# A graph attention layer on one core: p and the turned one-hots as float32r words in two parts, in place of three bf16 parts

## The chip, the cores and the metric
The kernel runs on one core of one Trainium2 chip. A core has five engines with instruction streams of their own: TensorE (PE; its weight loads are listed as PEld), VectorE (DVE), ScalarE (ACT), GpSimd (POOL) and SyncE (SP), which here only issues DMAs. They meet through semaphores. The metric is the device time of one execution in microseconds, lower is better.

## The reference
One layer over a graph of 12500 nodes with 256 features and 200000 edges (src, dst, weight), with 4 heads of 64 features. For each head:

```python
feats = jnp.maximum(x @ w1 + bb1, 0.0) @ w2 + bb2
x_cat = jnp.concatenate([feats[row], feats[col], elem[:, None]], axis=1)   # 64 + 64 + 1 = 129
hid = jnp.maximum(x_cat @ a1 + aab1, 0.0)
e1 = leaky_relu((hid @ a2 + aab2)[:, 0], 0.2)
w = jnp.exp(e1 - jnp.max(e1))
pooled = segment_sum(w[:, None] * feats[col], row, n)
row_sum = segment_sum(w, row, n) + 1e-10
return pooled / row_sum[:, None]
```

The heads are put side by side, added to x, and each row is normalised. Everything is float32.

## The kernel before, in words
The product with a1 is split. For each node the kernel makes p = feats @ a1[0:64] + ab1 (the part of the source node, 4 heads x 129 = 516 numbers, `ZW`) and q = feats @ a1[64:128] (of the destination). For an edge, hid is then relu(p[src] + q[dst] + weight * a1[128]).

**Set-up and sort stage** (up to about 1500 us). Edges are sorted by window: the source node number modulo 100 is the window (`W` = 100 windows of `WN` = 125 nodes). DVE makes one-hots of places (`chunks`, L1433) and row numbers (`row_ids`, L1442, L1447), PE multiplies them, POOL scatters the rows to memory (L695). Woven into the same loop by the lists `beside` and `order`, PE makes the node products, and for each window DVE adds the bias to p (`p_sum`, L1454), and POOL splits the f32 row of p into three bf16 rows that add up to it (`split_p`: cast L706, subtract L708, cast L711, subtract L713); SP stores them in `p_table` (L527), q and feats in `qf_table`.

**A passage** (1500 to some 1560 us). DVE makes small tables on one partition: `win_pack` (the window of each tile, four to a word) and `end_prev` (how many tiles must be done before a window of p may be overwritten), L1502 to L1511. It also splits the weight row a1[128] in three parts (`a_parts`, L1479 to L1487), which SP puts under each window of p as rows 125 to 127. PE turns the sorted records in 13 groups (L939), ACT and DVE take them, and ACT sets the accumulator `acc` to zero in 13 pieces (L1147). SP then loads the first records (L581) and raises `s_start`, for which PE, ACT, DVE and POOL wait.

**Tile loop** (to about 4700 us). 1664 tiles of 128 edges, 8 to a step, 3 steps to a body, in the order that `step` of each engine writes out. Per tile:
- POOL gathers the 128 rows of q and feats by an indirect DMA (L754).
- ACT builds the one-hot of each edge's source row in its window, with the edge weight in three bf16 parts in columns 125 to 127 (`onehots`, L1193 to L1197). PE turns it (`turn`, L984, in halves of four tiles), and ACT copies the turned half from PSUM to `onehot_t` as bf16 (`take_turned`, L1182).
- PE picks p[src] + weight * a1[128] by `onehot_t` times the three parts of the window `p_win`: three matmuls for each of two halves of 258 columns (`hidden_src`, L971). For the second half it also adds the gathered q in f32 (L975).
- DVE adds the q of the first half (L1558) and makes the four dots with a2 (L1568); once per step it makes the running maximum with PE's help (L1590, PE L990, L1594, PE L995, L1604).
- ACT scales the gathered feats by exp (`weight`, L1164, four per tile), PE sums them by source row with the unturned one-hot in f32 (`sum_up`, L958), and DVE adds the sums to `acc` (L1617).

PSUM has two buffers for the sums of p and q, two for L958's and one for the turn. SP reloads the two slots of `p_win` in turn: it waits until the tiles of the window before last are done (`s_z_mm`), loads (L594), waits for the landing (L595) and raises `s_win_ready`.

**Finish** (the last 130 us): division, x added, normalisation, output.

Of the kernel before, what the change touches and what calls it, by code (L numbers as in the profile page):

```python
# [25 lines left out]
I32 = mybir.dt.int32  # L26
BF16 = mybir.dt.bfloat16
AX_X = mybir.AxisListType.X


def gnn_layer(nc, x, src, dst, weight, W1, b1, W2, b2, A1, ab1, A2, ab2, out):
# [50 lines left out]
    p_table = nc.dram_tensor("p_table", (N, 3 * ZW), BF16, kind="Internal").ap()  # L82
# [7 lines left out]
    with ctx:  # L90
# [12 lines left out]
        ones_b = sb("ones_b", [P, P], BF16)  # L103
        before = sb("before", [P, P], BF16)
        iota_row = sb("iota_row", [P, WN])
        iota_win = sb("iota_win", [P, CH, W], BF16)
# [4 lines left out]
        onehot_t = sb("onehot_t", [P, SB, P], BF16)  # L111
# [13 lines left out]
        end_prev = sb("end_prev", [1, W], I32)  # L125
        win_pack = sb("win_pack", [1, NT // 4], I32)
# [4 lines left out]
        row_tmp = onehot_t[0:1, :, :].rearrange("p t n -> p (t n)").bitcast(I32)[:, 0:NT // 4]  # L131
        assert NT <= RING * P
# [17 lines left out]
        h_t = carve(MC * NG).rearrange("p (m n) -> p m n", m=MC)  # L150
        f_t = carve(2 * NG).rearrange("p (q n) -> p q n", q=2)
        p_f = carve(2 * ZW).rearrange("p (b n) -> p b n", b=2)
        p_out = carve(2 * 3 * ZW // 2).bitcast(BF16).rearrange("p (b n) -> p b n", b=2)
        qf_acc = carve(3 * QW)
        a_row = carve(ZW)
        a_rest = carve(ZW)
        a_parts = carve(3 * ZW // 2 + 2).bitcast(BF16)[:, 0:3 * ZW]
# [10 lines left out]
        hi_oh = carve(2 * HB * HI // 2).bitcast(BF16).rearrange("p (b c n) -> p b c n", b=2, c=HB)  # L168
        lo_oh = carve(2 * HB * LO // 2).bitcast(BF16).rearrange("p (b c n) -> p b c n", b=2, c=HB)
        same_col = carve(HCOL * LO).rearrange("p (c n) -> p c n", c=HCOL)  # L170
# [25 lines left out]
        base_lo = base_hl[:, CB * W // 2:].bitcast(BF16)  # L196
        edge_row = base_hl[:, 0:EC]
# [19 lines left out]
        before_f = carve_z(P)  # L217
        counts = carve_z(W)
# [13 lines left out]
        step_p = carve_z(3 * (W + 1)).bitcast(BF16).rearrange("p (u n) -> p u n", u=3)  # L232
        assert used_z[0] <= RING * QW
# [7 lines left out]
        p_flat = p_win[:, :, :].rearrange("p a n -> p (a n)")  # L241
        shift_flat = shift_all[:, :, :].rearrange("p s h -> p (s h)")
# [48 lines left out]
        s_acc_zero = sem("s_acc_zero")  # L291

# [13 lines left out]
        s_p_rest = sem("s_p_rest")  # L306
        s_p_mid = sem("s_p_mid")
# [175 lines left out]
        def _(sp):  # L483
# [71 lines left out]
            for v in range(2):  # L555
                for a, b in ROWS:
                    sp.dma_start(p_win[a:b, v, :], p_w[0:1, v, a:b, :].rearrange("a p n -> (a p) n")).then_inc(s_win[v], 16)
            sp.wait_ge(s_a_step, 5)
            for slot in range(2):
                for r in range(3):  # L560
                    sp.dma_start(p_win[WN + r:WN + r + 1, slot, :], a_parts[0:1, :]).then_inc(s_a_rows, 16)
# [17 lines left out]
            sp.wait_ge(s_tab_step, N_TAB_STEPS)  # L579
            sp.wait_ge(s_rec_st, 16 * BULK)  # L580
# [7 lines left out]
            with sp.Fori(1, W // 2) as g:  # L588
                for v in range(2):
# [3 lines left out]
                    for a, b in ROWS:  # L593
                        sp.dma_start(p_win[a:b, v, :], p_w[bass.ds(g, 1), v, a:b, :].rearrange("a p n -> (a p) n")).then_inc(s_win[v], 16)  # L594
# [24 lines left out]
        def _(pool):  # L619
# [5 lines left out]
            pool.memset(ones_b[:, :], 1.0).then_inc(s_const, 1)  # L625
# [5 lines left out]
            pool.iota(iota_win[:, :, :], [[0, CH], [1, W]], base=0, channel_multiplier=0, allow_small_or_imprecise_dtypes=True).then_inc(s_const, 1)  # L631
# [7 lines left out]
            pool.affine_select(out=before[:, :], in_=ones_b[:, :], pattern=[[1, P]], compare_op=ALU.is_ge,  # L639
# [4 lines left out]
            pool.tensor_copy(before_f, before[:, :]).then_inc(s_const, 1)  # L644
# [13 lines left out]
            pool.affine_select(out=before[:, :], in_=before[:, :], pattern=[[0, P]], compare_op=ALU.is_ge,  # L658
# [40 lines left out]
            def split_p(g, w):  # L699
# [86 lines left out]
        def _(pe):  # L786
# [158 lines left out]
            def step(i, k):  # L945
# [15 lines left out]
                def hidden_src(j):  # L961
# [67 lines left out]
        def _(act):  # L1029
# [16 lines left out]
            def windows(g, b, j):  # L1046
# [3 lines left out]
                for c in range(j * CH, (j + 1) * CH):  # L1050
                    op = act.activation(win_oh[0:EP, b % 2, c, :], iota_win[0:EP, 0, :], ACT.Abs, scale=-1.0,  # L1051
                                        bias=edge_win[0:EP, bass.ds((g * PER + b) * CB + c, 1)])
# [679 lines left out]
```

## Time and profile before

| | us |
|---|---|
| time, median of 3 runs | 4868.68 (4866.79 to 4869.52) |
| span of the profiled execution | 4828.3 |
| DVE busy | 4460.2 (92%) |
| PE busy | 4260.4 (88%) |
| ACT busy | 3835.5 (79%) |
| POOL busy | 2693.5 (56%) |

The profiled execution is known by its span, from its first to its last instruction; the time of a run also has what lies around that. Matmuls overlap in PE's pipeline, so the sum of their durations is more than PE's busy time. An f32 product shows as two entries (x2), a bf16 one as one. Line numbers are those of the kernel before.

### The profile page before, as it was taken

How to read it: one execution, taken by the hardware profiler on the slowest of the kernel's cores; microseconds unless marked ns; L12 is line 12 of the kernel's file. 1: busy time of each engine (PE TensorE's matmuls, PEld its weight loads, DVE VectorE, ACT ScalarE, POOL GpSimd, SP SyncE). 2: the span in 40 equal slices, each digit the busy share in tenths (PEclk: the TensorE clock that was granted, in tenths of full speed). 3: DMA queues.
4: the chain of work that ended last, by engine and by line, in shares of the span. 5: the costliest groups of instructions: out<-in, count | busy, mean ns of one | idle time of the engine just before them, and what ended most of it. 6: DMA issues, size and time to landing. Idle time of an engine off the chain costs nothing.

```text
span 4828.3 us, 133194 instructions
## 1 busy us (share of the span) xinstructions
PE 4260.4 (88%) x24114; PEld 3004.1 (62%) x24115; DVE 4460.2 (92%) x25378; ACT 3835.5 (79%) x12983; POOL 2693.5 (56%) x2886
## 2 busy tenths in 40 slices
PE   1598998898896999999999999999999999999990
PEld 1355555555555777777777777777777777777760
DVE  8799999999996999999999999999999999999998
ACT  1587778778774888888888888888888888888884
POOL 5366666666664555555555555555555555555544
PEclk9999999999997999999999999999999999999995
DMA  2133333333334877777777777777777777777757
GB/s 85 43 73 86 79 71 80 81 77 80 79 76 137 240 225 221 228 225 224 224 225 224 225 225 221 226 224 224 225 224 224 224 225 225 225 225 225 221 172 212
DMA packets 266918, 851.82 MB, mean 176 GB/s; under 512 B 107916, under 2 KB 109584, under 8 KB 266861
## 3 DMA queue, kind: packets, MB, share of 16 engines
q0 software_dynamic: 169920, 673.54, 50.0%
q1 hardware_dynamic: 63543, 160.18, 11.2%
q10 hardware_dynamic: 33398, 17.49, 1.4%
q8 instruction: 18, 0.29, 0.0%
q14 instruction: 39, 0.32, 0.0%
HBM read 739.10 MB, written 111.90 MB: 176 GB/s over the span
## 4 chain that ended last, share of the span: by engine, by line
PE 36%; ACT 27%; issue 3%; DVE 2%; DMA 1%; ACTq 0%; POOL 0%; DVEq 0%; SPq 0%; POOLq 0%
ACT z L1164 18%; PE psum L971 15%; PE psum L975 9%; PE psum L958 8%; ACT onehot L1193 3%; ACT onehot_t L1182 3%; PE psum L984 3%; ACT onehot L1197 2%; PE psum L939 1%; DVE z L1689 1%; DVE z L1682 0%; PE psum L995 0%; ACT onehot L1195 0%; DVE z L1705 0%; DMA p_win<-p_table 0%
## 5 line engine op out<-in xcount | busy, mean ns | idle before, releaser
L754 POOL DMA_INDIRECT z<-qf_table,rec x1664 | 1609.2, 967 | 1454.9 <-PE psum L958 1027.1
L1164 ACT ACTIVATE z<-z 128x64 f32<-128x64 f32 x6656 | 1651.1, 335 | 0.0
L971 PE MATMUL psum<-p_win,onehot_t 128*128 x9984 | 1407.8, 274 | 84.1 <-ACT onehot_t L1182 68.3
L971 PEld LDWEIGHTS psum<-p_win,onehot_t 128*128 128x128 bf16 x9984 | 966.8, 97 | 540.0 <-issue 214.4
L958 PE MATMUL psum<-z,onehot 128*128 128x260 f32 x3328 | 1029.4, 391 | 6.7 <-DVE acc L1617 4.9
L975 PE MATMUL psum<-z,ident 128*128 128x258 f32 x3328 | 1002.7, 383 | 0.0
L1568 DVE SCALAR_TENSOR_TENSOR z<-z,a_b 128x129 f32<-128x129 f32 x3328 | 884.3, 290 | 5.6 <-issue 0.2
L1568 DVE SCALAR_TENSOR_TENSOR z<-psum,a_b 128x129 f32<-128x129 f32 x3328 | 828.2, 286 | 0.0
L1558 DVE TENSOR_TENSOR z<-z,psum 128x258 f32<-128x258 f32 x1664 | 698.6, 420 | 94.6 <-PE psum L975 90.6
L1617 DVE TENSOR_TENSOR acc<-acc,psum 125x260 f32 x1664 | 702.3, 422 | 25.3 <-PE psum L958 2.4
L695 POOL DMA_INDIRECT sorted_rows<-z x300 | 478.5, 1595 | 403.9 <-DVE z L1447 321.6
L958 PEld LDWEIGHTS psum<-z,onehot 128*128 128x128 f32 x3328 | 575.8, 190 | 103.1 <-DVE acc L1617 27.7
L1182 ACT ACTIVATE onehot_t<-psum 128x512 bf16<-128x512 f32 x416 | 243.4, 585 | 437.7 <-PE psum L984 437.7
L1193 ACT ACTIVATE onehot<-iota_row,rec 128x125 f32<-128x125 f32 x1664 | 525.5, 389 | 26.3 <-PE psum L958 22.7
L1051 ACT ACTIVATE z<-iota_win,z 125x100 bf16<-125x100 bf16 x1600 | 470.3, 369 | 71.3 <-DMA base_rows<-z 56.3
L1433 DVE TENSOR_SCALAR acc<-z 125x320 bf16<-125x320 bf16 x1600 | 521.1, 388 | 0.3 <-issue 0.3
L975 PEld LDWEIGHTS psum<-z,ident 128*128 128x128 f32 x3328 | 502.2, 190 | 20.3
L857 PE MATMUL psum<-acc 128*128 128x500 f32 x800 | 377.8, 594 | 5.6 <-ACT acc L1085 5.6
L1398 DVE SCALAR_TENSOR_TENSOR z<-psum,z 125x100 f32<-125x100 f32 x1600 | 319.5, 253 | 24.1 <-PE psum L823 24.0
L984 PE MATMUL psum<-ident,onehot 128*128 128x128 f32 x1664 | 261.5, 280 | 55.7 <-ACT onehot L1197 55.7
L1197 ACT ACTIVATE onehot<-onehot,ones_f 128x500 f32<-128x500 f32 x416 | 298.2, 717 | 0.0
L1091 ACT ACTIVATE acc<-psum,acc 128x500 f32<-128x500 f32 x200 | 135.3, 676 | 196.0 <-PE psum L857 195.9
(220 smaller groups left out, 5576.3 us busy)
## 6 DMA issues: line engine op xcount, KB each, us to landing
p_table<-acc SPq DMA_DIRECT2D x100, 338.6 KB
p_win<-p_table SPq DMA_DIRECT2D x100, 338.6 KB
z<-qf_table,rec POOLq DMA_INDIRECT x1664, 4.5
qf_table<-acc SPq DMA_DIRECT2D x75, 339.5 KB
acc<-in_x_dram SPq DMA_DIRECT2D x25, 448.0 KB
z<-in_x_dram SPq DMA_DIRECT2D x20, 560.0 KB
out_dram<-z ACTq DMA_DIRECT2D x20, 560.0 KB
qf_table<-z SPq DMA_DIRECT2D x25, 339.5 KB
```

The source lines that it names most:

```text
L695: pool.indirect_dma_start(out=sorted_rows, out_offset=bass.IndirectOffsetOnAxis(ap=row_i[0:KB[k], (b - 3) % 2, k:k + 1], axis=0), in_=rows ...
L754: pool.indirect_dma_start(out=z_t[:, o + j, :], out_offset=None, in_=qf_table, in_offset=bass.IndirectOffsetOnAxis(ap=rec[:, o + j, 3:4].b ...
L958: pe.matmul(psum[:, 4 + j % 2, 0:H * HF], onehot[:, slot, :], z_t[:, slot, ZW:QW], start=True, stop=True)\
L971: mm = pe.matmul(to, onehot_t[:, j, :], p_flat[:, bass.ds((w % 2) * (3 * ZW) + (part * ZW + o), n)], start=(part == 0), stop=(part == 2 an ...
L975: mm = pe.matmul(z_two(slot), ident[:, :], z_t[:, slot, NA:ZW], start=False, stop=True, skip_group_check=True)
L1051: op = act.activation(win_oh[0:EP, b % 2, c, :], iota_win[0:EP, 0, :], ACT.Abs, scale=-1.0, bias=edge_win[0:EP, bass.ds((g * PER + b) * CB ...
L1164: op = act.activation(z_t[:, slot, o:o + DO], z_t[:, slot, o:o + DO], ACT.Copy, scale=z_t[:, slot, o + DO:o + HF])
L1193: op = act.activation(onehot[:, oo + j, 0:WN], iota_row[:, :], ACT.Abs, scale=-1.0, bias=rec[:, oo + j, 0:1])
L1433: op = dve.tensor_scalar(chunk_oh[0:EP, r, c, :], iota_k[0:EP, :], chunk_f[0:EP, c:c + 1], None, ALU.is_equal)
L1558: dve.tensor_tensor(own, own, z_one(slot), ALU.add).then_inc(s_z_added, 1)
L1568: return dve.scalar_tensor_tensor(out=own, in0=of, scalar=0.0, in1=a2_b[:, h * AT:(h + 1) * AT], op0=ALU.max, op1=ALU.mult, accum_out=e_ra ...
L1617: dve.tensor_tensor(a, a, psum[0:WN, 4 + j % 2, 0:H * HF], ALU.add).then_inc(s_acc, 1)
```

## The change
The three bf16 parts of p become two f32 words, written as float32r; the turned one-hot is stored as float32r too, and the matmul of each half runs over two parts. `p_table` and `p_win` hold 2 x 516 words of four bytes in a row (4128 bytes) where they held 3 x 516 of two (3096). POOL splits p by one cast and one subtract, DVE the weight row likewise. To make room, tables and constants move: `ones_b`, `before` and `iota_win` into space in z, the digit one-hots into that of h_t, and `win_pack` and `end_prev` are made in z and then stored by one DMA into partition 125 of `acc`, after ACT has zeroed it.

```diff
-        p_win = sb("p_win", [P, 2, 3 * ZW], BF16)
+        p_win = sb("p_win", [P, 2, 2 * ZW], F32R)
-        onehot_t = sb("onehot_t", [P, SB, P], BF16)
+        onehot_t = sb("onehot_t", [P, SB, P], F32R)
-        end_prev = sb("end_prev", [1, W], I32)
-        win_pack = sb("win_pack", [1, NT // 4], I32)
+        tables = acc[WN:WN + 1, 0:NT // 4 + W].bitcast(I32)
+        win_pack = tables[:, 0:NT // 4]
+        end_prev = tables[:, NT // 4:NT // 4 + W]
...
             sp.wait_ge(s_a_rows, 16 * 6)
             sp.wait_ge(s_tab_step, N_TAB_STEPS)
+            sp.wait_ge(s_acc_zero, 1 + BULK)
+            sp.dma_start(tables, made).then_inc(s_tab_st, 16)
+            sp.wait_ge(s_tab_st, 16)
             sp.wait_ge(s_rec_st, 16 * BULK)
...
-                pool.tensor_copy(p_out[0:WN, b, 0:ZW], pf).then_inc(s_p_hi, 1)
+                pool.tensor_copy(p_out[0:WN, b, 0:ZW].bitcast(F32R), pf).then_inc(s_p_hi, 1)
                 pool.wait_ge(s_p_hi, n + 1)
-                pool.tensor_tensor(pf, pf, p_out[0:WN, b, 0:ZW], ALU.subtract).then_inc(s_p_rest, 1)
-                pool.wait_ge(s_p_rest, n + 1)
-                pool.sem_inc(s_passed, 1)
-                pool.tensor_copy(p_out[0:WN, b, ZW:2 * ZW], pf).then_inc(s_p_mid, 1)
-                pool.wait_ge(s_p_mid, n + 1)
-                pool.tensor_tensor(p_out[0:WN, b, 2 * ZW:3 * ZW], pf, p_out[0:WN, b, ZW:2 * ZW], ALU.subtract).then_inc(s_p_lo, 1)
+                pool.tensor_tensor(p_out[0:WN, b, ZW:2 * ZW].bitcast(F32R), pf, p_out[0:WN, b, 0:ZW], ALU.subtract).then_inc(s_p_lo, 1)
...
-                        for part in range(3):
-                            mm = pe.matmul(to, onehot_t[:, j, :], p_flat[:, bass.ds((w % 2) * (3 * ZW) + (part * ZW + o), n)],
-                                           start=(part == 0), stop=(part == 2 and not (o and PEH)), skip_group_check=True)
+                        for part in range(2):
+                            mm = pe.matmul(to, onehot_t[:, j, :], p_flat[:, bass.ds((w % 2) * (2 * ZW) + (part * ZW + o), n)],
+                                           start=(part == 0), stop=(part == 1 and not (o and PEH)), skip_group_check=True)
...
-            dve.tensor_copy(ap3[:, 0, :], ar).then_inc(s_a_step, 1)
+            dve.tensor_copy(ap2[:, 0, :].bitcast(F32R), ar).then_inc(s_a_step, 1)
             dve.wait_ge(s_a_step, 1)
-            dve.tensor_tensor(rest, ar, ap3[:, 0, :], ALU.subtract).then_inc(s_a_step, 1)
-            dve.wait_ge(s_a_step, 2)
-            dve.tensor_copy(ap3[:, 1, :], rest).then_inc(s_a_step, 1)
-            dve.wait_ge(s_a_step, 3)
-            dve.tensor_tensor(rest, rest, ap3[:, 1, :], ALU.subtract).then_inc(s_a_step, 1)
-            dve.wait_ge(s_a_step, 4)
-            dve.tensor_copy(ap3[:, 2, :], rest).then_inc(s_a_step, 1)
+            dve.tensor_tensor(ap2[:, 1, :].bitcast(F32R), ar, ap2[:, 0, :], ALU.subtract).then_inc(s_a_step, 1)
```

## Rows read from the trace of the kernel before

**Rows 1.** The page, part 1: busy us (share of the span) x instructions.
```profile
PE 4260.4 (88%) x24114; PEld 3004.1 (62%) x24115; DVE 4460.2 (92%) x25378; ACT 3835.5 (79%) x12983; POOL 2693.5 (56%) x2886
```

**Rows 2.** Busy time by stage: stretch, its length, engines, PEclk, DMA share, GB/s.
```profile
200.00:1500.00 1300.00, 1152.51 (x4726) 661.03 (x4724) 1232.94 (x6178) 1004.52 (x2716) 826.85 (x696) 0.97 0.36 79
...
1600.00:4700.00 3100.00, 2966.46 (x18665) 2244.95 (x18665) 2898.40 (x18268) 2653.40 (x9860) 1681.98 (x2044) 1.00 0.76 223
```

**Rows 3.** The page, part 4: the chain that ended last, by engine.
```profile
PE 36%; ACT 27%; issue 3%; DVE 2%; DMA 1%; ACTq 0%; POOL 0%; DVEq 0%; SPq 0%; POOLq 0%
```

**Rows 4.** The chain in order of time, 3002 to 3018: start, us, what.
```profile
3009.05 0.52 PE psum L984 x4
...
3014.43 0.66 PE psum L971 x6
3015.09 0.44 PE psum L975 x2
...
3017.06 0.45 PE psum L984 x4
...
3017.61 0.60 ACT onehot_t L1182
```

**Rows 5.** ACT in order of time, 3002 to 3009: start, us [idle before].
```profile
3002.54 0.60 ACT L1182 ACTIVATE onehot_t<-psum 128x512 bf16<-128x512 f32 x1 [2.19 <-PE psum L984]
...
3008.14 0.72 ACT L1197 ACTIVATE onehot<-onehot,ones_f 128x500 f32<-128x500 f32 x1
```

**Rows 6.** Groups, 1600 to 4700: busy us, mean ns | idle before, releaser.
```profile
L971 PEld LDWEIGHTS psum<-p_win,onehot_t 128*128 128x128 bf16 x9840 | 952.1, 97 | 528.5 <-issue 207.3
...
L975 PEld LDWEIGHTS psum<-z,ident 128*128 128x128 f32 x3282 | 494.7, 190 | 20.1
...
L1182 ACT ACTIVATE onehot_t<-psum 128x512 bf16<-128x512 f32 x409 | 239.2, 585 | 420.5 <-PE psum L984 420.5
L984 PEld LDWEIGHTS psum<-ident,onehot 128*128 128x128 f32 x1636 | 188.1, 141 | 141.0 <-ACT onehot L1197 119.3 <-issue 0.3
```

**Rows 7.** Groups of DVE alone, 1600 to 4700.
```profile
L1558 DVE TENSOR_TENSOR z<-z,psum 128x258 f32<-128x258 f32 x1641 | 688.9, 420 | 81.0 <-PE psum L975 77.5 <-issue 0.5
...
L1594 DVE TENSOR_REDUCE head_max<-psum 4x1 f32<-4x128 f32 x206 | 57.1, 277 | 64.6 <-PE psum L990 64.6
```

**Rows 8.** Waits of SP, 1600 to 4600: us in total, times, longest.
```profile
SPq L594 <- PE psum L975: 2209.6, 96, 26.1
SPq L596 <- DMA p_win<-p_table: 499.5, 97, 6.4
```

**Rows 9.** Groups in the sort stage, 200 to 1500.
```profile
L1433 DVE TENSOR_SCALAR acc<-z 125x320 bf16<-125x320 bf16 x1576 | 515.5, 389 | 0.3 <-issue 0.3
...
L1442 DVE SCALAR_TENSOR_TENSOR z<-z 128x101 f32<-128x101 f32 x300 | 118.0, 441 | 7.2 <-ACT z L1079 7.1
L708 POOL TENSOR_TENSOR acc<-acc 125x516 f32<-125x516 f32 x100 | 115.4, 1154 | 8.3
L713 POOL TENSOR_TENSOR acc<-acc 125x516 bf16<-125x516 f32 x100 | 112.6, 1126 | 8.0
...
L711 POOL CAST acc<-acc 125x516 bf16<-125x516 f32 x100 | 61.9, 619 | 16.8 <-POOL acc L708 16.8
```

**Rows 10.** L1433 and L1442 in 200 to 1500: ns min/median/max.
```profile
L1433 DVE TENSOR_SCALAR acc<-z x1576: 286/298/1231, 199.7 to 1488.5; 125x320 bf16<-125x320 bf16 x197
...
L1442 DVE SCALAR_TENSOR_TENSOR z<-z x300: 308/316/1252, 217.2 to 1497.4; 128x101 f32<-128x101 f32 x150
```

**Rows 11.** POOL and DVE in order of time, 702 to 704.
```profile
702.72 1.10 POOL L713 TENSOR_TENSOR acc<-acc 125x516 bf16<-125x516 f32 x1
702.82 1.12 DVE L1442 SCALAR_TENSOR_TENSOR z<-z 128x101 f32<-128x101 f32 x1
```

**Rows 12.** ACT in order of time, 1550 to 1556.
```profile
1550.49 1.85 ACT L1147 ACTIVATE acc<-zero_col 128x2000 f32<-128x2000 f32 x1
```

**Rows 13.** The chain in order of time, its longest pieces.
```profile
1551.74 2.00 DMA records<-z
```

More of the change, by code:

```diff
@@ L27 @@
 BF16 = mybir.dt.bfloat16
+F32R = mybir.dt.float32r
 AX_X = mybir.AxisListType.X
@@ L81, in gnn_layer @@
     qf_table = nc.dram_tensor("qf_table", (N, QW), F32, kind="Internal").ap()
-    p_table = nc.dram_tensor("p_table", (N, 3 * ZW), BF16, kind="Internal").ap()
+    p_table = nc.dram_tensor("p_table", (N, 2 * ZW), F32, kind="Internal").ap()
     CHUNKS = NT * P // S
@@ L196, in gnn_layer @@
         base_lo = base_hl[:, CB * W // 2:].bitcast(BF16)
+        assert NT // 4 + W <= CB * W
+        made = base_hl[0:1, 0:NT // 4 + W].bitcast(I32)
+        made_pack = made[:, 0:NT // 4]
+        made_end = made[:, NT // 4:NT // 4 + W]
         edge_row = base_hl[:, 0:EC]
@@ L217, in gnn_layer @@
         before_f = carve_z(P)
+        ones_b = carve_z(P // 2).bitcast(BF16)
+        before = carve_z(P // 2).bitcast(BF16)
+        iota_win = carve_z(W // 2).bitcast(BF16)
         counts = carve_z(W)
@@ L624, in _ @@
             pool.memset(ones_f[:, :], 1.0).then_inc(s_const, 1)
-            pool.memset(ones_b[:, :], 1.0).then_inc(s_const, 1)
+            pool.memset(ones_b, 1.0).then_inc(s_const, 1)
             pool.memset(ident[:, :], 0.0).then_inc(s_const, 1)
@@ L630, in _ @@
             pool.iota(iota_row[:, :], [[1, WN]], base=1, channel_multiplier=0, allow_small_or_imprecise_dtypes=True).then_inc(s_const, 1)
[L631 removed]
+            pool.iota(iota_win, [[1, W]], base=0, channel_multiplier=0, allow_small_or_imprecise_dtypes=True).then_inc(s_const, 1)
             pool.iota(iota_k, [[1, KC_MAX]], base=-(KC_MAX // 2), channel_multiplier=0, allow_small_or_imprecise_dtypes=True).then_inc(s_const, 1)
@@ L637, in _ @@
                                fill=1.0, base=0, channel_multiplier=1).then_inc(s_const, 1)
-            pool.affine_select(out=before[:, :], in_=ones_b[:, :], pattern=[[1, P]], compare_op=ALU.is_ge,
+            pool.affine_select(out=before, in_=ones_b, pattern=[[1, P]], compare_op=ALU.is_ge,
                                fill=0.0, base=-1, channel_multiplier=-1).then_inc(s_const, 1)
@@ L643, in _ @@
             pool.tensor_copy(ident_b, ident[:, :]).then_inc(s_const, 1)
-            pool.tensor_copy(before_f, before[:, :]).then_inc(s_const, 1)
+            pool.tensor_copy(before_f, before).then_inc(s_const, 1)
             pool.affine_select(out=same_col, in_=ones_f[:, 0:HCOL * LO].rearrange("p (c n) -> p c n", c=HCOL), pattern=[[-HI, HCOL], [0, LO]],
@@ L657, in _ @@
             pool.wait_ge(s_const, 17)
-            pool.affine_select(out=before[:, :], in_=before[:, :], pattern=[[0, P]], compare_op=ALU.is_ge,
+            pool.affine_select(out=before, in_=before, pattern=[[0, P]], compare_op=ALU.is_ge,
                                fill=1.0, base=EP - 1, channel_multiplier=-1).then_inc(s_const, 1)
@@ L1050, in windows @@
                 for c in range(j * CH, (j + 1) * CH):
-                    op = act.activation(win_oh[0:EP, b % 2, c, :], iota_win[0:EP, 0, :], ACT.Abs, scale=-1.0,
+                    op = act.activation(win_oh[0:EP, b % 2, c, :], iota_win[0:EP, :], ACT.Abs, scale=-1.0,
                                         bias=edge_win[0:EP, bass.ds((g * PER + b) * CB + c, 1)])
@@ L1501, in _ @@
             table_steps = [
-                lambda: dve.tensor_copy(win_pack[:, :], quarter[:, 0, :]),
+                lambda: dve.tensor_copy(made_pack, quarter[:, 0, :]),
                 lambda: dve.tensor_scalar(row_tmp[:, :], quarter[:, 1, :], 7, None, ALU.logical_shift_left),
-                lambda: dve.tensor_tensor(win_pack[:, :], win_pack[:, :], row_tmp[:, :], ALU.bitwise_or),
+                lambda: dve.tensor_tensor(made_pack, made_pack, row_tmp[:, :], ALU.bitwise_or),
                 lambda: dve.tensor_scalar(row_tmp[:, :], quarter[:, 2, :], 14, None, ALU.logical_shift_left),
-                lambda: dve.tensor_tensor(win_pack[:, :], win_pack[:, :], row_tmp[:, :], ALU.bitwise_or),
+                lambda: dve.tensor_tensor(made_pack, made_pack, row_tmp[:, :], ALU.bitwise_or),
                 lambda: dve.tensor_scalar(row_tmp[:, :], quarter[:, 3, :], 21, None, ALU.logical_shift_left),
-                lambda: dve.tensor_tensor(win_pack[:, :], win_pack[:, :], row_tmp[:, :], ALU.bitwise_or),
-                lambda: dve.memset(end_prev[:, :], 1),
-                lambda: dve.tensor_scalar(end_prev[:, 2:W], ends[0:1, 0:W - 2], 1.0 / P, 1.0, ALU.mult, ALU.add),
+                lambda: dve.tensor_tensor(made_pack, made_pack, row_tmp[:, :], ALU.bitwise_or),
+                lambda: dve.memset(made_end, 1),
+                lambda: dve.tensor_scalar(made_end[:, 2:W], ends[0:1, 0:W - 2], 1.0 / P, 1.0, ALU.mult, ALU.add),
                 lambda: dve.tensor_scalar(sizes[:, :], ends[:, :], 1.0 / P, -1.0, ALU.mult, ALU.add),
```

40 lines of the change are left out of this document (20 added, 20 removed).

## The prediction, made before the changed kernel was run
> **What bounds the kernel now.** I first read the page's busy shares, which settle little: PE 88%, DVE 92%, ACT 79% [rows 1]. The table by stage says more. The sort stage takes 1300 us and is DVE's, busy for 1233 of them; a passage of 100 us follows; the tile loop takes 3100 us of the 4828, and there PE is busy 2966, DVE 2898, ACT 2653, with the granted clock at its full level, 2.4 GHz [rows 2]. Three engines are close together in the loop, so its bound has to be read from the chain of waits.
>
> The page's chain is mostly PE and ACT, hardly DVE [rows 3]. In order of time it goes round once in 8 tiles (a step; 208 of them) [rows 4, 5]. From 3002.54 ACT copies a half of the turned one-hots, scales 16 quarter rows, builds four one-hots and ends with L1197 at 8.14 + 0.72 = 3008.86. PE's turn L984 waits for that and starts at 3009.05 or just before; then PE does four tiles and the next turn, and at 3017.61 ACT's L1182 starts again, having waited for it. The ring is 15.07 us: some 6.4 of ACT and 8.7 of PE. 3100 us over 206 steps [rows 2, 7] are 15.05 each, so the ring is the step. In PE's part each tile is six matmuls of the changed line in 0.66 us (110 ns each, 258 columns), then an f32 product with ident in 0.44, and the f32 sum over a one-hot in as much [rows 4].
>
> What stands just behind the ring is DVE: in the loop it waited for PE 77.5 us before L1558 and 64.6 us before L1594, 142 us together [rows 7]. That is all the loop can shrink before DVE is never without work. POOL, busy 1682 of 3100 [rows 2], has room.
>
> **The change part by part.**
>
> (1) Tile loop, PE. Per tile six bf16 matmuls become four float32r ones of the same 258 columns: two fewer. No row shows float32r, so its price lies between rows. Low end: the bf16 row, 110 ns a matmul [rows 4]; 4 × 0.11 = 0.44 for 0.66, −0.22 us a tile. Middle: the f32 row, where one f32 product is two entries in 0.44, so one entry with 258 columns takes 0.22; 4 × 0.22 = 0.88, +0.22 a tile. High end: a whole f32 product each, 4 × 0.44 = 1.76, +1.10 a tile. I take the low end: an f32 product needs two entries of double length, that is four times the bf16 matmul, because it takes both operands at full precision, and the change splits p into two words so that one pass for each will do. Each matmul also loads its stationary one-hot, now 4-byte words. The bf16 load takes 97 ns, an f32 load 190 or, for the turns, 141 [rows 6]; yet four turns with four f32 loads run in 0.44 to 0.52 us [rows 4], 0.11 to 0.13 each, so loads of 4-byte words do overlap, at about the pace of a bf16 matmul.
>
> The Trainium skill speaks against the change here: "TensorE: Matmul & The Clock Gate", section "Weight-path perf modes — Fast Weight Load (FWL) and DoubleRow", says that the fast load is on for 128 weights of a type other than FP32, and its LDWEIGHTS section gives columns over 1.2, so 107 ns for 128 columns as an estimate. The loads above agree in direction (97 against 141 and 190 ns). By that rule, overlapped, the four still take 4 × 0.11; were load and matmul one after the other it would be 4 × 0.215 = 0.86, the middle case.
>
> In the ring PE's part has four of those tiles: 4 × 0.22 = 0.88 us a step, over 208 steps 183 us if nothing else held. DVE's 142 us is the ceiling. Both are near each other: after −0.68 a step DVE has no idle time left, and the turn still waits for ACT's L1197, because ACT's part is unchanged, so the L990 that L1594 waits for stays partly late. I take 130 us (0.63 a step, nine tenths of the ceiling); bounds 50 and 160 (142 plus some of DVE's short gaps).
>
> (2) Tile loop, ACT. L1182 writes 128x512 words of four bytes instead of two. Its 585 ns [rows 6] are for 512 columns; L1197 writes 500 columns of f32 in 717 [rows 5] by another function, so the bound is +0.13. I take 0; it would add at most 0.13 to the ring a step (27 us), inside the bounds.
>
> (3) Tile loop, DMA. A window of p grows from 3096 to 4128 bytes a row. SP waited 499.5 us for 97 loads, 5.1 us each, behind which stands only the next window's load; but it waited 2209.6 us for PE before them, 23 us each [rows 8]. A third more is 1.7 us, hidden by the 23. The extra bytes, 129 KB in 31 us, are 4 GB/s on 223, at a DMA share of 0.76 [rows 2]. Nothing; the DMA share rises to about 0.8 with the faster loop.
>
> (4) Sort stage, POOL. A split goes from cast, subtract, cast, subtract (L706, L708, L711, L713) to cast, subtract. POOL has time there, so its own time is not the point. The point is DVE: L1433 has a median of 298 ns, a least of 286 and a longest of 1231, L1442 316 and 1252 [rows 10]. At 702.82 an L1442 takes 1.12 us and ends with POOL's L713, which ran from 702.72 to 703.82 [rows 11]: DVE was held behind a POOL instruction. Over the stage L1433 has 1576 × (389 − 298) = 143 us above its median, L1442 300 × (441 − 316) = 37 [rows 9, 10]: 180 us, in a stage of which DVE is busy 95%. The Trainium skill has a rule for such a pair: "SBUF — State Buffer", section "A bandwidth-pool intuition that's wrong (but worth ruling out)", says that GpSimd and a DVE two-port operation cannot run at once and one fully blocks; it describes POOL as the one that waits, and here DVE does too.
> A cast (619 ns) and a subtract (1126) go, a cast and a subtract stay [rows 9]: half, 90 us of the 180, if all of it came from the split. Some comes from POOL's scatters, and DVE now idles a little more on PE. I take 65; bounds 20 and 95. The kept subtract writes four-byte words: L708 with an f32 result against L713 with bf16 is 1154 and 1126 ns [rows 9], so no dearer. p_table's rows grow by a third; SP's stores are far below a DMA share of 0.36 [rows 2]. In the same way POOL's last splits before the last scatters give the passage about 2 us.
>
> (5) The passage. DVE's five steps on one row become two, off the path, since the chain there goes over POOL's scatters and the 13 field groups. Added: SP, in order, waits for ACT's last zeroing (L1147 from 1550.49 for 1.85, so 1552.34), stores the table row and waits for it, before the load of the first records, which now goes when the last record store has landed, at 1551.74 + 2.00 = 1553.74 [rows 12, 13]. Behind it on SP is that load and then the start of all engines. The table's store takes about as long as that one, so 1552.34 + 0.3 + 2.0 = 1554.6. Cost +1 us; bounds 0 and 3. Table reads by the sequencers from the other row are the same instruction. Smaller masks in the set-up: nothing, under 0.5 us on POOL.
>
> **Sum.** −130 − 65 − 2 + 1 = −196 us. The profiled span is 4828.3; what lies around it, 4868.7 − 4828.3 = 40.4, stays. The profiled execution has no time of its own beside its span, and the three runs lie within 2.7 us, so I take the span to be that of the median run: 4868.7 − 196 = 4673.
>
> **The rivals.**
> (a) DVE and ACT hold the loop. PE comes round early, and then waits on the sums, on s_z_free and on L1197, which all keep their pace; the interplay of three near-equal engines eats most of it. For it: DVE 2898 of 3100 busy, PE already waits 119 us before the turn's load for L1197 [rows 6]. Against: in the ring DVE isn't on the chain. Loop −50: 4869 − 50 − 66 = 4753.
> (b) POOL's relief doesn't reach the end, DVE's held time being replaced by waits for PE (busy 1152 of 1300). Loop −130 alone: 4738.
> (c) The other side: float32r words stream at the f32 pace, 0.22 us for 258 columns. Place: L971 in the ring; it decides as soon as a float32r matmul takes over 0.165 us, since four then cost more than six. +0.22 × 4 × 208 = +183, less 66: 4986. For it: every four-byte operand that the traces show moves at 0.22 us for 258 columns. Against: each of those is a full-precision product, two entries.
> (d) float32r isn't granted a shorter path at all, each word a whole f32 product: +1.10 × 1664 = +1830, so 6633. The change would then not do what it says.
>
> The Trainium skill sides against (c) and (d): "FP8 and Floating Point Precision", section "TensorE Precision Notes", lists a reduced-precision FP32 that reads four bytes and truncates, beside true FP32 in four passes. The true part agrees with the rows (0.44 is four times 0.11); the other no trace of before shows.
>
> **How the numbers follow.** Forecast 4673, chance 0.61, own range 4620 to 4735. (a) 0.17, (b) 0.05, (c) 0.11, (d) 0.04; 0.02 for a float32r matmul near 0.165 us with the POOL gain lost as well, which is no change. A change of under 0.2% (10 us) can't be told from none. Faster: 0.61 + 0.17 + 0.05 = 0.83, and 0.01 more from values between (a) and (c): 0.84. Same 0.02, slower 0.14. The range leaves out (c) and (d) and a little of the fast end: 4605 (loop −160, sort −95, and a few us) to 4790 (loop −50, sort −20 and some).
>
> **What would show it.** L971 with some 6656 matmuls, each six-for-0.66 piece of the chain now four for 0.44; a step of about 14.4 us; DVE's waits for PE under 50 us, and DVE on the chain. L1182 near 585 ns. L1433's mean near 345 ns and L713's counterpart near 1130; the sort stage about 65 us shorter. L594's DMA 6 to 7 us, with SP still waiting for PE over 20 us before each. It is wrong if the four take 0.66 us or more, if ACT's waits before L1182 vanish while DVE's stay, or if the sort stage keeps its 1300 us.

## The result, and the profile after

| | time, median (runs), us | ratio to the kernel before, 95% interval |
|---|---|---|
| kernel before | 4869.1 (4866.79 to 4870.23) | |
| changed kernel | 4758.2 (4755.32 to 4760.98) | 0.9774 (0.976 to 0.9787) |

The change saves 111 us, 2.3%. Forecast were 196: the time lies inside the range (4605 to 4790), outside the likeliest case's own (4620 to 4735).

The profiled execution took 4755.32 us and spans 4753.6. First the page of the changed kernel, its busy times and its chain by engine, which answer to [rows 1] and [rows 3]:

```profile
PE 4012.7 (84%) x20786; PEld 2950.1 (62%) x20787; DVE 4394.5 (92%) x25375; ACT 3821.9 (80%) x12983; POOL 2562.5 (54%) x2686
...
ACT 37%; PE 20%; issue 7%; DVE 3%; ACTq 1%; DMA 1%; another core or an unknown queue 0%; POOL 0%; DVEq 0%; SPq 0%; POOLq 0%
```

3328 matmuls are gone and PE is busy 248 us less; on the chain PE fell from 36% to 20% and ACT rose from 27% to 37% (the next profile of the kernel before, below, has 31% and 18%). DVE, which was forecast to be on it, has 3%.

Then the groups of 1600 to 4600, with busy us, mean ns | idle before. They answer to [rows 6] and [rows 7]; L978 was L971, L1189 L1182, L991 L984, L1559 L1558, L1595 L1594:

```profile
L978 PE MATMUL psum<-p_win,onehot_t 128*128 x6480 | 1310.4, 324 | 122.0 <-ACT onehot_t L1189 78.8 <-issue 25.3 <-DVE z L1569 14.9
...
L978 PEld LDWEIGHTS psum<-p_win,onehot_t 128*128 128x128 f32 x6480 | 976.0, 188 | 371.9 <-issue 302.0
...
L1559 DVE TENSOR_TENSOR z<-z,psum 128x258 f32<-128x258 f32 x1620 | 676.8, 418 | 40.1 <-PE psum L982 21.6 <-issue 14.3 <-remote 1.4
...
L991 PE MATMUL psum<-ident,onehot 128*128 128x128 f32 x1620 | 253.8, 279 | 150.9 <-ACT onehot L1204 137.6 <-issue 13.3
L1189 ACT ACTIVATE onehot_t<-psum 128x512 fp32r<-128x512 f32 x405 | 237.6, 587 | 365.7 <-PE psum L991 239.0 <-issue 113.6 <-PE psum L982 13.1
...
L1595 DVE TENSOR_REDUCE head_max<-psum 4x1 f32<-4x128 f32 x203 | 56.4, 278 | 50.0 <-PE psum L997 41.4 <-issue 7.1
```

PE waits for ACT in two places: 138 us before the turn (for the one-hots, L1204) and 79 us before L978 (for the copy of the turned half, L1189). It did so in the kernel before as well. These are its two rows on the page, over the whole span of the profile shown ahead, and the second wait is the longer one there:

```profile
L984 PE MATMUL psum<-ident,onehot 128*128 128x128 f32 x1664 | 261.5, 280 | 55.7 <-ACT onehot L1197 55.7
...
L971 PE MATMUL psum<-p_win,onehot_t 128*128 x9984 | 1407.8, 274 | 84.1 <-ACT onehot_t L1182 68.3
```

The sort stage, 200 to 1450, same columns, answers to [rows 9]; L1440 was L1433, L1449 L1442, L720 L708:

```profile
L1440 DVE TENSOR_SCALAR acc<-z 125x320 bf16<-125x320 bf16 x1573 | 503.6, 382 | 0.3 <-issue 0.3
...
L720 POOL TENSOR_TENSOR acc<-acc 125x516 fp32r<-125x516 f32 x100 | 134.8, 1348 | 8.3
...
L1449 DVE SCALAR_TENSOR_TENSOR z<-z 128x101 f32<-128x101 f32 x294 | 80.0, 320 | 0.0
```

L1449's mean fell from 441 to 320 ns, 4 above its median of 316; L1440's only from 389 to 382. The last L1440 starts at 1449.5. The last L1433 started at 1488.5 in the profile shown ahead and at 1489.5 in the next one.

**Where the 111 us went.** For this the kernel before needs a profile of an ordinary execution. The one shown ahead spans 4828.3, and the next spans 4866.5 (below). The instruction that comes once a step, the reduction of the maximum, gives the rest; each row is one kernel (again before, then changed), with count, ns min/median/max, and first and last start:

```profile
L1594 DVE TENSOR_REDUCE head_max<-psum x208: 273/279/280, 1599.8 to 4735.0; 4x1 f32<-4x128 f32 x104
```
```profile
L1595 DVE TENSOR_REDUCE head_max<-psum x208: 271/278/280, 1562.1 to 4622.9; 4x1 f32<-4x128 f32 x104
```

The first came 37.7 us earlier: 40.0 from the sort stage, less 2.3 that the passage and the start of the loop lost. The 207 steps between first and last took 3060.8 us for 3135.2, 74.4 less: a mean step of 14.79 for 15.15. Together 112.1 of the 112.9 by which the spans differ. All step times are such means, last start less first over 207, where they are not called medians. Some of the expectations speak of the median step instead, from one of these starts to the next: it is 15.08 in the kernel before and 14.69 in the changed one, under the mean because some steps are much longer than the rest.

### The profile page after: what moved, and what is told of

Read it like the earlier page. It is cut to its first block, busy times and chain, and to the rows that moved or that the text cites. A ratio compares the mean times of both kernels' runs of the same rounds, so it can differ in the third digit from the quotient of the medians.

```text
span 4753.6 us, 122909 instructions
## 1 busy us (share of the span) xinstructions
PE 4012.7 (84%) x20786; PEld 2950.1 (62%) x20787; DVE 4394.5 (92%) x25375; ACT 3821.9 (80%) x12983; POOL 2562.5 (54%) x2686
## 4 chain that ended last, share of the span: by engine, by line
ACT 37%; PE 20%; issue 7%; DVE 3%; ACTq 1%; DMA 1%; another core or an unknown queue 0%; POOL 0%; DVEq 0%; SPq 0%; POOLq 0%
ACT z L1171 24%; PE psum L978 7%; ACT onehot L1200 6%; PE psum L982 5%; PE psum L965 5%; ACT onehot_t L1189 4%; ACT onehot L1204 3%; PE psum L991 2%; PE psum L946 1%; DVE z L1690 1%; ACTq L1209 1%; ACT onehot L1202 1%; DVE z L1569 1%; DVE z L1683 0%
## 5 line engine op out<-in xcount | busy, mean ns | idle before, releaser
L978 PE MATMUL psum<-p_win,onehot_t 128*128 x6656 | 1348.0, 324 | 146.4 <-ACT onehot_t L1189 80.9
L978 PEld LDWEIGHTS psum<-p_win,onehot_t 128*128 128x128 f32 x6656 | 1004.1, 189 | 406.1 <-issue 334.5
L1559 DVE TENSOR_TENSOR z<-z,psum 128x258 f32<-128x258 f32 x1664 | 695.2, 418 | 76.0 <-PE psum L982 33.8
L1189 ACT ACTIVATE onehot_t<-psum 128x512 fp32r<-128x512 f32 x416 | 244.2, 587 | 407.8 <-PE psum L991 271.5
L1058 ACT ACTIVATE z<-z 125x100 bf16<-125x100 bf16 x1600 | 470.3, 369 | 68.7 <-DMA base_rows<-z 56.3
L982 PEld LDWEIGHTS psum<-z,ident 128*128 128x128 f32 x3328 | 514.7, 189 | 0.7 <-issue 0.7
L1440 DVE TENSOR_SCALAR acc<-z 125x320 bf16<-125x320 bf16 x1600 | 509.8, 380 | 0.3 <-issue 0.3
L991 PE MATMUL psum<-ident,onehot 128*128 128x128 f32 x1664 | 261.5, 280 | 161.4 <-ACT onehot L1204 148.1
L991 PEld LDWEIGHTS psum<-ident,onehot 128*128 128x128 f32 x1664 | 192.0, 141 | 264.8 <-ACT onehot L1204 221.4
L1204 ACT ACTIVATE onehot<-onehot,ones_f 128x500 f32<-128x500 f32 x416 | 298.1, 716 | 0.0
```

The source lines that it names most:

```text
L982: mm = pe.matmul(z_two(slot), ident[:, :], z_t[:, slot, NA:ZW], start=False, stop=True, skip_group_check=True)
L991: mm = pe.transpose(psum[:, 6, j * P:(j + 1) * P], onehot[:, ((k + off) * SB + u * HALF_SB + j) % RING, :], ident[:, :])
L1440: op = dve.tensor_scalar(chunk_oh[0:EP, r, c, :], iota_k[0:EP, :], chunk_f[0:EP, c:c + 1], None, ALU.is_equal)
L1559: dve.tensor_tensor(own, own, z_one(slot), ALU.add).then_inc(s_z_added, 1)
```

## The experiments

**1. The kernel before, again.** No edit.

> The kernel before, unchanged, profiled once more. Its first profile spans 4828.3 us while its timed runs take 4869, 41 us more; the changed kernel spans 4753.6 and takes 4755 to 4761. Theory A: executions of the kernel before hold stalls of some 40 us that the first profile happened to lack (like the 15 and 7 us for which DVE sits idle at the start of the tile loop in the changed kernel's profile, and steps of 15.3 to 16.4 us among steps of 14.6); then this profile spans about 4865, with a loop start or steps longer than in the first. Rival B: what lies around the span is 41 us for this kernel, whatever the execution; then it spans 4828 again with all steps at 15.07 to 15.12 us.

4868.2 us, ratio 1.0001 (0.9991 to 1.0012), span 4866.5. So 1.7 us lie around the span, not 40; it was the first profiled execution that was 38 us short of the others. Of those, 22 us come before the first reduction (1577.6 in the profile ahead, 1599.8 here) and 14 in the steps (15.08 each, here 15.15). DVE in order of time shows the first part, start, us [idle before]:

```profile
1575.07 0.42 DVE L1558 TENSOR_TENSOR z<-z,psum 128x258 f32<-128x258 f32 x1 [8.66 <-remote]
```

Two more such waits, of 4.46 and 5.07 us, follow at 1580.81 and 1595.19. DVE stands idle for 18 us at the start of the loop, released by nothing that the profile names. The changed kernel has the same, 22 us of it:

```profile
1544.18 0.42 DVE L1559 TENSOR_TENSOR z<-z,psum 128x258 f32<-128x258 f32 x1 [15.15 <-remote]
...
1552.63 0.42 DVE L1559 TENSOR_TENSOR z<-z,psum 128x258 f32<-128x258 f32 x1 [7.18 <-remote]
```

**2. Only PE relieved: two bf16 parts.** The third part is left out of the sum.

```diff
-                        for part in range(3):
+                        for part in range(2):
```

> The kernel before with PE's third matmul of each half left out (the third bf16 part of p and of the weight row is not added), nothing else changed: four bf16 matmuls a tile. It gives the price of float32r by difference. Theory A (a float32r matmul costs what a bf16 one does, 0.11 to 0.12 us): the median step of the tile loop is that of the changed kernel, 14.6 to 14.7 us, and the whole is some 90 us under the kernel before (loop only, no relief in the sort stage): about 4780. Rival B (float32r words cost PE more than it seems, by the loads of four-byte words or the longer pipeline): the step is 14.3 or less, 4700.

4782.0 us, ratio 0.9827 (0.981 to 0.9843). The first reduction starts at 1601.4, the step is 14.72. Two bf16 matmuls fewer a tile are worth 88 us (4866.5 − 4778.0), all in the loop; with float32r the step is 14.79. So float32r itself costs 0.07 us a step, 14 us in all, and even four matmuls at the price of bf16 would not have brought 130.

**3. Only POOL relieved: two bf16 parts made.** The third part of `p_table` stays zero (its place in `p_out` is zeroed once, in the set-up).

```diff
-                pool.tensor_tensor(pf, pf, p_out[0:WN, b, 0:ZW], ALU.subtract).then_inc(s_p_rest, 1)
...
-                pool.tensor_tensor(p_out[0:WN, b, 2 * ZW:3 * ZW], pf, p_out[0:WN, b, ZW:2 * ZW], ALU.subtract).then_inc(s_p_lo, 1)
+                pool.tensor_tensor(p_out[0:WN, b, ZW:2 * ZW], pf, p_out[0:WN, b, 0:ZW], ALU.subtract).then_inc(s_p_lo, 1)
```

> The kernel before with POOL's split of p stopped after cast and subtract (the second part is written as bf16, the third is zero); tile loop unchanged. It isolates the relief of DVE in the sort stage. Theory A (DVE was held behind POOL's instructions): the stage is some 38 us shorter, as in the changed kernel (its loop starts 38 us earlier), L1433's mean falls under 389 ns and L1442's under 441; total about 4831. Rival B (the 38 us come from the moved tables and masks, not from POOL): the stage stays within 5 us, total 4869.

4820.9 us, ratio 0.9904 (0.9887 to 0.992). Groups of its sort stage (L1429 is the line of L1433, L709 of L708, L1438 of L1442):

```profile
L1429 DVE TENSOR_SCALAR acc<-z 125x320 bf16<-125x320 bf16 x1572 | 482.8, 369 | 0.3 <-issue 0.3
...
L709 POOL TENSOR_TENSOR acc<-acc 125x516 bf16<-125x516 f32 x100 | 116.0, 1160 | 8.3
...
L1438 DVE SCALAR_TENSOR_TENSOR z<-z 128x101 f32<-128x101 f32 x297 | 80.7, 320 | 0.9 <-issue 0.9
```

The first reduction comes at 1552.7, 47 us earlier than in the kernel before, where 38 were expected; the step stays 15.15. The two gains add up: 88 + 47 = 135, of which the change has 112; the missing 23 are the 14 of float32r in the loop and 9 before its first reduction. Some six of the nine are in the sort stage, where L720 takes 1348 ns for L709's 1160 and L1440's mean is 382 for L1429's 369. The moved tables and masks, which this kernel doesn't have, are thus not where the sort stage's gain comes from.

**4. and 5. What a float32r matmul costs: eight matmuls a tile.** The products of some parts are added twice, bf16 in the kernel before, float32r in the changed one, so that PE sets the step in both. In bf16 it is the first part that is added twice.

```diff
-                        for part in range(2):
+                        for part in range(4):
-                            mm = pe.matmul(to, onehot_t[:, j, :], p_flat[:, bass.ds((w % 2) * (2 * ZW) + (part * ZW + o), n)],
-                                           start=(part == 0), stop=(part == 1 and not (o and PEH)), skip_group_check=True)
+                            mm = pe.matmul(to, onehot_t[:, j, :], p_flat[:, bass.ds((w % 2) * (2 * ZW) + (part % 2 * ZW + o), n)],
+                                           start=(part == 0), stop=(part == 3 and not (o and PEH)), skip_group_check=True)
```

> The kernel before with eight bf16 matmuls a tile in L971 instead of six (the first part is added twice; the output is not the reference's). It makes PE the longest: 8 tiles x (0.88 + 0.44 + 0.44) + 1.3 = 15.4 us a step and the waits; the ring grows by 4 x 0.22 = 0.88 to 15.95. Both theories of the float32r price expect a median step of 15.9 to 16.3 us here.

> The changed kernel with eight float32r matmuls a tile instead of four (each part added twice; the output is not the reference's). Theory A (a float32r matmul of 258 columns holds PE 0.12 us against 0.11 for bf16): the step is that of the eight bf16 ones plus about 8 x 8 x 0.01 = 0.6 us if PE is the bound, 16.3 to 16.9. Rival B (the same price): within 0.1 us of bf16_eight. Rival C (0.13 and more when the addresses come from registers): 17.2 or above.

5009.3 us, ratio 1.0292 (1.0272 to 1.0313), and 5057.3, ratio 1.0391 (1.037 to 1.0412). A piece of the chain in order of time, bf16 and then float32r (start, us, what):

```profile
3001.52 0.88 PE psum L971 x8
```
```profile
3000.24 0.96 PE psum L978 x8
```

110 and 120 ns each. By the steps, 15.82 and 16.23 us with 64 such matmuls in each, the difference is 0.41 / 64 = 6 ns. PE is 64% and 66% of the two chains, and each kernel was timed twice only. Both prices are far from the 165 ns at which four would cost as much as six.

**6. ACT's order.** In a step ACT copies the second turned half, builds four one-hots, weighs tile 0, copies the next first half, weighs tiles 1 to 4, builds four one-hots, weighs 5 to 7, and only then comes the copy of the next second half (`take_turned(0, 1)`, at the top of the next step), for which PE's fifth tile waits. The edit moves that copy ahead of two of those tiles' scalings:

```diff
-                if live(i, k, 0):
-                    take_turned(0, 1)
...
+                    if j == SB // 2 + 1 and live(i, k, 1):
+                        take_turned(1, 1)
```

> The changed kernel with ACT's copy of the second turned half (L1189 for u = 1) moved up, from the start of the next step to behind the sixth of the eight scalings. Theory A (the loop is now held by ACT: after its one-hots come 12 scalings and only then this copy, for which PE's fifth tile waits): the median step falls from 14.70 to about 14.3 us, PE's waits for L1189 of 79 us vanish, total about 4700 to 4680. Rival B (the loop is held by DVE or by PE's own work and ACT's place is a coincidence): the step stays at 14.6 to 14.7, total 4755.

4738.1 us, ratio 0.9732 (0.9716 to 0.9749), 20 us under the changed kernel. PE's waits, 1600 to 4600:

```profile
L978 PE MATMUL psum<-p_win,onehot_t 128*128 x6518 | 1299.4, 321 | 56.9 <-issue 39.5 <-DVE z L1569 16.1
...
L991 PE MATMUL psum<-ident,onehot 128*128 128x128 f32 x1632 | 256.4, 280 | 125.3 <-ACT onehot L1204 118.0 <-issue 7.3
```

The 79 us for L1189 are gone, as they should be. But the median step went from 14.69 to 14.49, not to the 14.3 that was expected, the mean from 14.79 to 14.71, and the time missed the 4680 to 4700. Something else stands close behind. In 1600 to 4600 the chain now goes from ACT to PE by the one-hots, L1204, 95 times and never by the copy.

**7. The same move in the kernel before.**

> The kernel before with ACT's copy of the second turned half moved up behind the sixth scaling, as in act_order (4738 from 4758). Theory A (in the kernel before the copy's place was already a second ring beside the one over the one-hots, both at 15.1 us, so it also capped what fewer matmuls could give): the median step falls a little, 15.08 to about 14.9, and the time by 20 to 40 us. Rival B (before, only the ring over L1197 and the turn counted, and the copy became late only with the change): step 15.08, time the same within 10 us.

4824.0 us, ratio 0.9912 (0.9895 to 0.9929): 43 us less, more than in the changed kernel and just over the 20 to 40 expected. The wait was there before the change; this is the row of the kernel before, run again:

```profile
L971 PE MATMUL psum<-p_win,onehot_t 128*128 x9504 | 1340.9, 274 | 82.0 <-ACT onehot_t L1182 44.3 <-issue 21.6 <-DVE z L1568 5.8
```

With the move its L971 waits 28.3 us instead of 82.0, none of it put down to the copy.

**8. and 9. Is DVE the bound?** One of the four dots takes 1 column of 129 (the rest of head 0's is left out), in the changed kernel and in the one with the moved copy. DVE's busy time in 1600 to 4600 falls from 2844 to 2692 us.

```diff
+                    n = 1 if h == 0 else AT
-                    own = z_t[:, slot, h * AT:(h + 1) * AT]
+                    own = z_t[:, slot, h * AT:h * AT + n]
...
```

> The changed kernel with DVE's dot of the first head over 1 of its 129 columns (that part of the computation is left out): 8 x about 0.13 us less of DVE a step, about 1.1 us. Theory A (the loop of the changed kernel is held by ACT's order, its copy behind 12 scalings): the median step stays at 14.5 to 14.7, and the time within 40 us of 4758. Rival B (DVE holds it): the step falls by most of 1.1 us to 13.7, about 4560.

> The same shortened dot on top of the moved copy. Theory A (once ACT's copy is out of the way, DVE is the bound at 14.4 to 14.5 us a step): the step falls from 14.50 to the ring over ACT's one-hots and PE's four tiles, 13.7 to 14.0, the time from 4738 to about 4620. Rival B (that ring is itself the 14.5): the step stays within 0.1 us, about 4730.

| step, us (time) | all columns | one dot short |
|---|---|---|
| changed kernel | 14.79 (4758.2) | 14.80 (4759.5) |
| with the copy moved | 14.71 (4738.1) | 14.50 (4694.0) |

In the changed kernel some 0.7 us less for DVE in every step brings nothing: DVE is not its bound. With the copy moved it brings 44 us, which is neither the 4620 nor the 4730 that were expected; the median step fell from 14.49 to 14.22, where 13.7 to 14.0 or no change was expected. Ratios: 0.9754 (0.9738 to 0.9771) and 0.9621 (0.9605 to 0.9637). The kernel before took 4878.9 us beside these two and the next two, 12 us more than the 4867.0 beside the others, so a gain read from the ratios comes out some 0.2% larger (54 us for the 44). The steps within each profile, 14.80 for 14.79 and 14.50 for 14.71, say the same as the times.

**10. and 11. The idle time at the start of the loop.** POOL's gathers of the first steps wait for no sum. The edit lets them, from the second step's on, wait until the p and q of the tile one step earlier are summed; in the changed kernel, and with the copy moved as well.

```diff
+                    elif tile(1, j) >= SB:
+                        pool.wait_ge(s_z_mm, tile(0, j) + 2)
```

> The changed kernel, in whose first steps POOL's gathers of tiles 8 to 23 each wait until PE has done the tile eight before, as they do in effect later; before, 24 gathers go out back to back. In the profiles of the changed kernel, of the kernel before (second profile) and of the two-part bf16 variant the first two steps take 46.8 to 47.2 us, with DVE and ACT idle for up to 15 us while these 24 gathers run; in the first profile of the kernel before they take 25.3. Theory A (the burst of gathers causes that idle time): the first two steps fall to some 27 us and the time to about 4738. Rival B (it comes from something else at the loop's start, such as code that is fetched): 4758 and 47 us as before.

> Both edits together: ACT's copy of the second turned half moved up (it gave 4738) and the first gathers paced. If both are independent: 4738 less what pacing alone gives, so about 4718 with theory A of the pacing, 4738 with B.

4754.6 us, ratio 0.9745 (0.9729 to 0.9762), and 4739.3, ratio 0.9712 (0.9696 to 0.9729). By the ratio pacing brings 0.3% and 0.2%, by the time 4 us in the one and a loss of 1 in the other: next to nothing of the 20 that were expected. In the trace the first reduction comes at 1550.8 instead of 1562.1, and DVE's longest unexplained wait is 6.04 us instead of 15.15. So the gathers have to do with it. But the step grew, 14.84 for 14.79 and 14.78 for 14.71, and took it back: the last reduction starts at 4623.1 for 4622.9, and at 4610.8 for 4610.0. So the idle time at the start is not worth its length.

**12. The changed kernel, again.**

> The changed kernel unchanged, on the same chip as the others of this call. 0.977 of the kernel before; median step 14.7, first two steps 47 us, some 20 steps of 0.5 to 2 us over the median.

4758.4 us, ratio 0.9777 (0.9761 to 0.9794), first reduction at 1562.9, last at 4622.7. Two profiles of the changed kernel agree; the odd one is the first of the kernel before.

## Why the prediction was off in size

**The step that failed: the path, and with it the ceiling.** The prediction took ACT's last one-hot instruction, L1197, as what releases PE's turn at 3009.05, and PE's next four tiles as the rest of the ring. The rows don't show that. L1197 ends at 3008.86, so the one-hots come just in time, and PE in order of time has no idle time before this turn, which follows its own L975:

```profile
3008.45 0.60 PE L975 MATMUL psum<-z,ident 128*128 128x258 f32 x2
3008.91 0.66 PE L984 MATMUL psum<-ident,onehot 128*128 128x128 f32 x4
```

The chain is on PE's own work from 2999.91 to 3017.51, without a piece of ACT. In the very next step the same chain does turn from ACT to PE, and not by the one-hots (start, us, what):

```profile
3023.28 0.65 ACT onehot L1197
...
3026.79 0.48 ACT onehot_t L1182
...
3027.71 0.92 PE psum L971 x6
...
3032.69 0.60 ACT onehot_t L1182
```

In 1600 to 4600 of this profile PE waits for the copy L1182 130 times (64.8 us) and for L1197 132 times (45.5 us); the chain goes over all of the first and none of the second. In the ordinary profile, of the kernel before again, it goes over the copy 68 times and over L1197 26 times, in the changed kernel 83 and 39 times. That the ring came out at 15.07 us, as long as the mean step, was no proof of its path: every instruction that comes once a step returns after one step, whichever way the chain goes between. The price of four tiles for the ring was therefore four tiles of a path that this profile never takes.

The path over the copy, from [rows 4]'s L1182 at 3017.61 to the next at 3032.69, has 9.66 us of ACT, to the end of the second copy at 3027.27, and 5.42 of PE: three tiles, the turn and what lies between, 15.08 in all. The chain of the changed kernel in order of time (start, us, what):

```profile
3002.03 0.48 PE psum L978 x4
...
3004.30 0.61 PE psum L991 x4
...
3005.02 0.60 ACT onehot_t L1189
...
3014.20 0.48 ACT onehot_t L1189
...
3019.58 0.60 ACT onehot_t L1189
```

Six matmuls in 0.66 have become four in 0.48, near the 0.44 forecast. PE in order of time, [idle before], shows its waits for the one-hots and for the copy:

```profile
3011.39 0.66 PE L991 MATMUL psum<-ident,onehot 128*128 128x128 f32 x4 [0.55 <-ACT onehot L1204]
...
3015.11 0.76 PE L978 MATMUL psum<-p_win,onehot_t 128*128 x4 [0.53 <-ACT onehot_t L1189]
```

ACT's part is the same 9.66 us, 3005.02 to 3014.68, none of which the change touches. PE's three tiles and the turn then take 4.90 us for 5.42. Over the copy a step is 14.56 us for 15.08, so this path lets the loop shrink by 0.52 a step, an estimate of 108 us over 207 steps, where the prediction had 183 and DVE's 142. Experiments 6 and 7 show that this wait is real, and 8 that DVE isn't what holds the changed kernel.

**Term by term.**
- Loop, −130: measured −74, with a step of 14.79 where 14.4 was foreseen. I took DVE's 142 us of waiting as all that the loop can shrink and nine tenths of it as the gain. Half of it came, and DVE's waits for PE at L1559 and L1595 (63 us, where under 50 were foreseen) did not run out. Of the missing 56, the price of float32r has 14, since two bf16 parts give −88 (207 steps in 3046.9 us for 3135.2). For the other 42 the runs show less: moving the copy takes 17 us out of the loop of the changed kernel (3043.9 for 3060.8), and only then does a shorter dot of DVE take another 43. That these two are the 42 is argued, since no run moves the copy or shortens a dot with two bf16 parts. The path over the copy alone would allow more than came: 39 of the changed kernel's 207 steps are over 0.3 us longer than the median of 14.69, 32 us together (19 steps and 21 us in the kernel before again), and what makes them long no run here shows.
- float32r near the low end: right, 120 ns beside 110, where I chose 110 out of 110 to 440. −88 became −74 by it. Rivals (c) and (d) needed 165 ns and 440. The load of the one-hot takes 188 ns for 97, and they overlap with the matmuls: four in 0.48. The Trainium skill, "TensorE: Matmul & The Clock Gate", section "Weight-path perf modes — Fast Weight Load (FWL) and DoubleRow", leaves FP32 out of the fast load; the 188 ns of this load, which the trace lists as f32, agree with it. Taken one after the other, load and matmul would have made rival (c), and that the trace refutes.
- Sort stage, −65: measured −40. By the same count as in the prediction, DVE's held time is now 1573 × (382 − 298) + 294 × (320 − 316) = 133 us, 47 less than 180, where half, 90, were assumed. With two bf16 parts it is 1572 × (369 − 298) + 297 × (320 − 316) = 113, and the stage is 46 shorter. So of a removed us of held time most reaches the end (40 of 47, 46 of 67), and the amount that is removed was taken too large.
- Which of the held instructions were freed: all of L1442's 37 us went, but only 11 of L1433's 143. In the kernel before again 49 of the 53 long L1442 (over 0.42 us) overlap the removed L713, as [rows 11] had shown one. Of the 195 long L1440 of the changed kernel, 98 overlap one of the hundred kept subtracts, L720, and 62 a scatter. The Trainium skill's page "SBUF — State Buffer", section "Who interferes with whom", says that whichever of the two issues first has the port pair for the whole instruction. [rows 11] and the cleared L1442 agree with that, DVE being the second.
- The kept subtract, "no dearer": wrong, it takes 1348 ns against 1154, 19 us in a hundred, and with two bf16 parts, at 1160 ns, the held time is 20 us less. [rows 9] had compared an f32 result with a bf16 one, but both subtracts there had a bf16 input; now both inputs are f32 words. The result is float32r as well, and no run changes one without the other.
- Last splits and passage, −2 + 1: the last L1440 is 40.0 us earlier, the first reduction 37.7, a loss of 2.3 for a forecast gain of 1. The table's store itself was priced well: from the end of SP's issue of the last record stores to its load of the first records it is 2.22 us (1513.92 to 1516.14) for 1.74 in the kernel before again, +0.5 where +1 stood. The rest lies where DVE stands idle at the start of the loop, and the two profiles of the kernel before differ by 22 us up to their first reductions.
- ACT's copy, 0: right, 587 ns for 585.
- DMA, 0: right. SP's waits in 1600 to 4600:

```profile
SPq L606 <- PE psum L982: 1572.3, 72, 25.8
SPq L608 <- DMA p_win<-p_table: 283.4, 50, 7.2
```

The trace has a wait of SP at some of the loads only: 5.7 us each for 50 landings (5.1 before; 6 to 7 were foreseen) and 21.8 us each for 72 waits for PE, where over 20 were foreseen. The DMA share is 0.79 in these 3000 us, and the window's load has 13 us of the chain in 1600 to 4600 of both kernels' first profiles.
- What lies around the span, 40: wrong, it is 1.7. No term hung on it, since both kernels carry the same; had the next profile been the one shown, the step would have read 15.15 and not 15.07.

**The rivals.** (a) gave 4753 and is nearest to the 4758, but by luck: its loop of −50 and its sort stage of −66 stand against −74 and −38 up to the first reduction, and the two errors cancel. Of its mechanism, three near-equal engines, ACT's part is what runs and experiments show; DVE's is refuted for the changed kernel and comes true once the copy is moved. (b) fell: the two gains add up. The slow end of the range, loop −50 and sort −20, adds up to 4799 and not 4790, which changes nothing here. The range held the result because it was wide enough for (a) and (b); the likeliest case's own range, and the path behind it, did not.

**A better version.** The changed kernel with the copy moved, 4738.1 us, leaves nothing out and beats both.

**Open.** Moving the copy should have brought a median step of 14.3 and brought 14.49. The mean is 14.71 because 65 of the 207 steps are over 0.3 us longer than the median, 47 us together; a shorter dot lowers both (14.22 and 14.50) and does not remove these steps. What makes them long no run here explains. The idle time at the start of the loop, and why the first profiled execution of the kernel before had less of it.

## What to carry to other kernels

A loop's period proves no path: any instruction that comes once a step returns after one step. Before a ring is priced, look at each place where it turns from one engine to the other and see that the chain turns there, over several steps and not one; here the next ten microseconds of the same chain showed another turn, and the page its 68 us of waiting. For every other wait of the engine, follow the other engine's program order back to the last thing they exchanged. The idle time of one engine is at best a ceiling for what the loop can lose, never an estimate, and another path can lie below it. When an interfering engine's work is halved, look which of the hindered instructions the removed half meets, and profile the kernel before twice before its span is used.

## What the runs showed that was not expected

- A float32r matmul of 258 columns against 128x128 takes 0.12 us in the chain (bf16 0.11, a whole f32 product 0.44); its entry in the trace lasts 324 ns (bf16 274) and its load 188 (97).
- A POOL subtract of 125x516 with two inputs of f32 words and a float32r result takes 1348 ns, with one input bf16 1126 to 1160 (f32 or bf16 result).
- Two profiled executions of the kernel before, both with the clock granted in full in the loop, spanned 4828.3 and 4866.5 us; the slower agrees with the timed runs, 4866.79 to 4870.23.
- At the start of the loop DVE stands idle for up to 15 us at a time with nothing in the profile that releases it, and holding back the indirect gathers shortens that to 6 us.
